# Cross-attention on one core: G x by seven block products, with y's low parts later on GpSimd

## The reference

```python
x_q = jnp.einsum('oc,bcn->bno', w_qk, y)
x_k = jnp.einsum('oc,bcn->bon', w_qk, x)
x_v = jnp.einsum('oc,bcn->bon', w_v, x) + b_v[None, :, None]
energy = jnp.einsum('bnc,bcm->bnm', x_q, x_k)
attention = jax.nn.softmax(energy, axis=-1)
attention = attention / (1e-07 + attention.sum(axis=1, keepdims=True))
x_r = jnp.einsum('bcn,bnm->bcm', x_v, attention)
x_r = jax.nn.relu(jnp.einsum('oc,bcn->bon', w_t, x - x_r) + b_t[None, :, None])
return x + x_r
```

## Time and profile before

| | value |
|---|---|
| median of 3 runs | 1847.62 us (1847.48 to 1848.41) |
| profiled execution, span | 1846.8 us |
| PE busy | 1841.7 us, 100% |
| VectorE (DVE) busy | 1499.5 us, 81% |
| ScalarE (ACT) busy | 1310.9 us, 71% |
| GpSimd (POOL) busy | 788.0 us, 43% |
| bytes moved | 101.92 MB, mean 55 GB/s |

### The profile page before, as it was taken

The page is one execution under the profiler, slowest core; times in us unless marked ns, Lnnn a source line. Parts: engine busy times, 40 slices in busy tenths (PEclk is TensorE's granted clock), DMA queues, the critical chain, the costliest instruction groups (busy, mean ns, idle before and its releaser), DMA issues.

```text
span 1846.8 us, 26440 instructions
## 1 busy us (share of the span) xinstructions
PE 1841.7 (100%) x8901; PEld 1553.5 (84%) x8901; DVE 1499.5 (81%) x2034; ACT 1310.9 (71%) x1799; POOL 788.0 (43%) x422
## 2 busy tenths in 40 slices
PE   9999999999999999999999999999999999999999
PEld 8888888888888888888888888888888888888887
DVE  7878787787887877878878788787787877878777
ACT  7767776677666786667776677766677666776665
POOL 5543344432444424444244452444533444334431
PEclk9999999999999999999999999999999999999999
DMA  3201111011110111101111111111011110111101
GB/s 108 68 25 57 58 68 68 23 68 46 68 68 23 68 46 68 68 33 58 46 68 68 48 43 46 68 68 61 30 48 66 68 68 23 64 50 68 68 1 46
DMA packets 34090, 101.92 MB, mean 55 GB/s; under 512 B 4224, under 2 KB 5248, under 8 KB 34048
## 3 DMA queue, kind: packets, MB, share of 16 engines
q1 hardware_dynamic: 33760, 101.07, 15.8%
q10 hardware_dynamic: 288, 0.39, 0.1%
HBM read 67.90 MB, written 33.55 MB: 55 GB/s over the span
## 4 chain that ended last, share of the span: by engine, by line
PE 98%; DVE 1%; ACT 0%; issue 0%; POOL 0%; DVEq 0%; ACTq 0%; POOLq 0%
PE pv L796 37%; PE row_b L691 19%; PE row_a L691 14%; PE pv L768 9%; PE row_b L754 5%; PE row_a L754 5%; PE row_a L745 5%; PE row_b L745 5%; DVE colsum L536 0%; PE pv L898 0%; PE pv L754 0%; PE pv L931 0%; PE pv L902 0%; ACT p_sb L336 0%; DVE z_lo L503 0%
## 5 line engine op out<-in xcount | busy, mean ns | idle before, releaser
L218 POOL TENSOR_TENSOR y_lo<-y_raw,y_hi 128x896 fp32r<-128x896 f32 (+1 forms) x128 | 277.1, 2190 | 546.7 <-ACT y_hi L297 357.1
L543 DVE SCALAR_TENSOR_TENSOR p_lo<-p_sb,row_inv,p_hi 128x1024 fp32r<-128x1024 f32 x254 | 325.4, 1282 | 96.0 <-ACT p_hi L344 95.9
L327 ACT ACTIVATE ev<-row_b 128x512 f32<-128x512 f32 x384 | 229.5, 598 | 199.7 <-PE row_b L691 199.1
L203 POOL TENSOR_TENSOR x_lo<-x_sb,x_hi 128x1024 fp32r<-128x1024 f32 x63 | 152.2, 2415 | 449.2 <-ACT x_hi L280 449.2
L336 ACT ACTIVATE p_sb<-p_sb,neg_max 128x1024 f32<-128x1024 f32 x256 | 295.1, 1154 | 28.6 <-DVE neg_max L518 24.6
L344 ACT ACTIVATE p_hi<-p_sb,row_inv 128x1024 fp32r<-128x1024 f32 x256 | 292.4, 1143 | 30.7 <-PE pv L796 30.0
L536 DVE SCALAR_TENSOR_TENSOR colsum<-p_sb,row_inv,colsum 128x1024 f32<-128x1024 f32 x224 | 291.7, 1302 | 8.5 <-DVE row_inv L526 0.6
L796 PE MATMUL pv<-p_hi,z_hi 128*128 128x512 f32 x1024 | 273.7, 389 | 0.0
L796 PE MATMUL pv<-p_hi,z_lo 128*128 128x512 f32 x1024 | 273.7, 389 | 0.0
L518 DVE CUSTOM_DVE_ANT_0 p_sb<-row_a,ev 128x1024 f32<-128x1024 f32 x128 | 156.6, 1223 | 143.6 <-PE row_a L691 143.6
L796 PE MATMUL pv<-p_lo,z_hi 128*128 128x512 f32 (+1 forms) x1047 | 271.7, 383 | 0.0
(11 more groups left out here) (157 smaller groups left out, 3585.9 us busy)
## 6 DMA issues: line engine op xcount, KB each, us to landing
x_sb<-x SPq DMA_DIRECT2D x64, 512.0 KB, 4.6
out<-res SPq DMA_DIRECT2D x62, 512.0 KB, 3.4
y_raw<-y SPq DMA_DIRECT2D x64, 256.0 KB, 3.7
y_raw<-y SPq DMA_DIRECT2D x32, 512.0 KB, 3.7
out<-res SPq DMA_DIRECT2D x2, 256.0 KB, 2.1
res<-w_qk SPq DMA_DIRECT2D x1, 256.0 KB, 3.0
res<-w_t_T SPq DMA_DIRECT2D x1, 256.0 KB, 6.7
res<-w_v SPq DMA_DIRECT2D x1, 256.0 KB, 7.8
```

The source lines that it names most:

```text
L218: nc.gpsimd.tensor_tensor(y_lo[:, of:, cols], y_raw[:, 1 + of:8, cols], y_hi[:, of:, cols].bitcast(FP32), ALU.subtract).then_inc(y_lo_done, 1)
L327: nc.scalar.activation(ev[:, to, :], bank_b, ACT.Copy, scale=scale).then_inc(b_copied, 1)
L543: nc.vector.scalar_tensor_tensor(out=p_lo[r][:, :], in0=p_sb[r][:, :], scalar=row_inv[:, j:j + 1], in1=p_hi[r][:, :].bitcast(FP32), op0=AL ...
```

## The change

G x is computed by seven block products of three matmuls each, 21 matmuls of 512 columns where there were 24. For that:

- Once, in batch 0, ScalarE and GpSimd make seven 128 x 128 operands from G and their low parts (`g_operands_high`, `g_operands`). ScalarE's part stands in pair 0 ahead of the first exponentials, and its last instruction waits for all five of GpSimd's sums.
- Four sums of blocks of x are made by DMA: SyncE loads four blocks (`load_xt`) behind the next y, and GpSimd's queue issues three accumulating transfers (`xt_one`, `xt_two`, `xt_four`), each behind a wait for the one before. ScalarE makes their high parts (`xt_high`, in pairs 2 and 3), GpSimd their low parts (`xt_low`, two of 128 x 1024, behind the two `x_low`).
- The seven products stand among the last pair's `pv_pass`. Four PSUM copies on ScalarE (`gx_pass`) carry a partial result from bank to bank, and VectorE adds two (`gx_add`) ahead of `gx_parts`. PE waits for these copies at `gx_p6`, `gx_p3`, `gx_p7` and `gx_p4`. `gx_p5` waits for both `xt_low`.
- GpSimd makes `y_low` of tiles 1 to 3 last in its batch, behind `t_low`, and without the wait for the last `p_low`. `y_sums` of the next batch stands behind `xt_one`, which waits for the four x blocks.
- To make room, `x_sb` is single: x comes once into `x_raw` (over which `x_lo` is written) and again into `x_sb` (`keep_x`, behind the store of the batch before), and `x_bias` moves from pairs 0 and 1 to pairs 1 and 2. `turn` writes over `p_sb[0]` and `colsum`, and stands ahead of the last `p_low`. `scale(b, 1)` stands behind the first `z_low`.

```diff
+            def load_xt(b):
+                for block, kt, cols in ((X_T1, 0, left), (X_T3, 1, right), (X_T2, 1, right), (X_T4, 1, left)):
+                    sp.dma_start(xt_raw[:, block, :], x_dram[b][:, kt, cols]).then_inc(xt_in, DMA)
...
-                        load_x(b + 1, 1 - par, t)
+                        keep_x(b, t)
+                if not last:
+                    if not first:
+                        sp.wait_ge(w_done, KT * b)
+                    for kt in range(KT):
+                        load_x(b + 1, 1 - par, kt)
 
...
+            def xt_one(b):
+                pool.wait_ge(xt_in, 4 * DMA * b)
+                shared = x_dram[b][:, 0, right].rearrange("p (a n) -> p a n", a=1).to_broadcast([P, 2, BANK])
+                pool.dma_start(xt_raw[:, X_T1:X_T3 + 1, :], shared,
+                               accum_op=ALU.add).then_inc(xt1_added, DMA)
...
+            def xt_two(b):
+                pool.wait_ge(xt1_added, DMA * b)
+                pool.dma_start(xt_raw[:, X_T2, :], xt_raw[:, X_T1, :],
+                               accum_op=ALU.add).then_inc(xt2_added, DMA)
...
+            def xt_four(b):
+                pool.wait_ge(xt2_added, DMA * b)
+                pool.dma_start(xt_raw[:, X_T4, :], xt_raw[:, X_T2, :],
+                               accum_op=ALU.add).then_inc(xt4_added, DMA)
...
+            def xt_low(b, h):
+                pool.wait_ge(xt_hi_done, 2 * (b - 1) + h + 1)
+                two = slice(2 * h, 2 * h + 2)
+                nc.gpsimd.tensor_tensor(xt_lo[:, two, :], xt_raw[:, two, :],
+                                        xt_hi[:, two, :].bitcast(FP32), ALU.subtract).then_inc(xt_lo_done, 1)
...
                 if not last:
+                    xt_one(b + 1)
                     y_sums(b + 1)
+                    xt_two(b + 1)
+                    if b == 0:
+                        g_operands()
...
                     y_low(b + 1, 0)
+                    xt_four(b + 1)
                     for kt in range(KT):
                         x_low(b + 1, 1 - par, kt)
-                    pool.wait_ge(p_lo_done, NT * (b + 1))
-                    for t in range(1, NP):
-                        y_low(b + 1, t)
+                    for h in range(2):
+                        xt_low(b + 1, h)
                     t_three(b + 1)
                     t_low(b + 1, 0)
                     t_low(b + 1, 1)
-
-            nc.gpsimd.memset(zeros[:, :], 0.0).then_inc(zeros_made, 1)
+                    for t in range(1, NP):
+                        y_low(b + 1, t)
...
+            def xt_high(b, h):
+                if h == 0:
+                    act.wait_ge(xt1_added, DMA * b)
+                else:
+                    act.wait_ge(xt4_added, DMA * b)
+                two = slice(2 * h, 2 * h + 2)
+                nc.scalar.activation(xt_hi[:, two, :], xt_raw[:, two, :],
+                                     ACT.Copy).then_inc(xt_hi_done, 1)
...
+                act.wait_ge(g_summed, 5)
+                nc.scalar.activation(gs_hi[:, G_S1:G_NS4 + 1, :], g_sums, ACT.Copy).then_inc(gs_hi_done, 1)
...
+            def gx_pass(b, to, of, done, count, scale):
+                act.wait_ge(done, count)
+                nc.scalar.activation(to, of, ACT.Copy, scale=scale).then_inc(gx_passed, 1)
...
                 if t >= 2 and not last:
                     x_high(b + 1, 1 - par, t - 2, early=first)
+                    xt_high(b + 1, t - 2)
...
+                if t == 0 and first:
+                    g_operands_high()
...
-                if t < 2 and not first and (t == 1 or not last):
-                    x_bias(b, par, t)
-                if t == 0 and last:
+                if 0 < t < 3 and not first and (t == 2 or not last):
+                    x_bias(b, t - 1)
+                if t == 1 and last:
...
+                if t == NP - 1 and not last:
+                    gx_pass(b + 1, gx11, gx22, gx22_part, 3 * b + 1, -1.0)
+                    gx_pass(b + 1, ev[:, 3, :], gx12, gx12_part, b + 1, 1.0)
+                    gx_pass(b + 1, ev[:, 2, :], gx22, gx22_part, 3 * b + 2, 1.0)
                 if t == NP - 1:
                     p_high(b, t, 1, first)
...
+                    gx_high_one(b + 1)
+                    gx_pass(b + 1, gx21, gx22, gx22_part, 3 * b + 3, -1.0)
                     y_high(b + 1, 2)
-                    gx_high(b + 1)
+                    y_high(b + 1, 3)
+                    gx_high_two(b + 1)
```

```diff
+            def gx_add(b):
+                dve.wait_ge(gx12_full, b)
+                dve.wait_ge(gx_passed, 4 * b - 1)
+                nc.vector.tensor_tensor(gx12, gx12, ev[:, 2, :], ALU.add).then_inc(gx_added, 1)
+                dve.wait_ge(gx_passed, 4 * b)
+                nc.vector.tensor_tensor(gx22, gx22, ev[:, 3, :], ALU.add).then_inc(gx_added, 1)
...
                 if b < B - 1 or t < NP - 1:
                     p_low(b, t, 0)
+                if b < B - 1 and t == NP - 1:
+                    turn(b)
+                if b < B - 1 or t < NP - 1:
                     p_low(b, t, 1)
...
+                gx_add(b + 1)
                 gx_parts(b + 1)
                 col_inverse(b)
                 scale(b, 0)
+                z_low(b + 1, 0)
                 scale(b, 1)
-                z_low(b + 1, 0)
                 z_low(b + 1, 1)
...
+            def gx_p5(b):
+                pe.wait_ge(xt_lo_done, 2 * b)
+                pe.wait_ge(gs_lo_done, 1)
+                sum_product(gx12, G_S1, X_T1, True).then_inc(gx12_part, 1)
...
+            def gx_p6(b):
+                pe.wait_ge(gx_passed, 4 * b - 3)
+                sum_product(gx22, G_NS2, X_T2, False).then_inc(gx22_part, 1)
...
+            def gx_p4(b):
+                pe.wait_ge(gx_passed, 4 * b)
+                sum_product(gx21, G_22, X_T4, False).then_inc(gx21_full, 1)
...
-                for n in range(3):
-                    pv_pass(b, t - 1, 1, n)
+                if t == NP - 1 and not last:
+                    pv_pass(b, t - 1, 1, 0)
+                    gx_p1(b + 1, 1 - par)
+                    gx_p5(b + 1)
+                    pv_pass(b, t - 1, 1, 1)
+                    gx_p6(b + 1)
+                    gx_p2(1 - par)
+                    pv_pass(b, t - 1, 1, 2)
+                    gx_p3(b + 1, 1 - par)
+                    gx_p7(b + 1)
+                    pv_pass(b, t, 0, 0)
+                    gx_p4(b + 1)
+                else:
+                    for n in range(3):
+                        pv_pass(b, t - 1, 1, n)
...
-                    next_pair(b, t, first)
-                if not last:
-                    pe.wait_ge(x_lo_done, KT * (b + 2))
-                    pe.wait_ge(max_done, NT * (b + 1))
-                    for k in range(4):
-                        g_block(1 - par, k)
```

198 lines of the change are left out of this document (143 added, 55 removed).

## The result

The changed kernel takes **2258.16 us** (median of 4 runs, 2255.38 to 2259.35), the one before 1847.6 beside it: ratio 1.2221, 95% interval 1.2203 to 1.2238. It is 22% slower. I had said 2127, from 1975 to 2230: the direction is right, the time is above the range. The profiled execution spans 2253.6 us.

What follows compares the result with a forecast made beforehand. PE, busy 1841.7 of 1846.8 us, was taken as the bound. A batch: -0.68 + 4.2 + 4.4 + 0.6 = +8.5 us, 255 in 30 batches; batch 0 adds 24: 2126, with 0.8 2127 us; range 1975 to 2230.

Steps and rivals of the forecast that it cites:

- Full price of a wait: On PE, busy 1841.7 of 1846.8 us: every new wait of PE costs its full length.
- B: At gx_p5, PE waits for GpSimd's two xt_low: 3.95 us, 4.4 in steady batches; bounds 2.65 and 4.0.
- A: At the next batch's first y_high, y's sums on GpSimd come 5.7 us late; PE waits 4.2, bounds 1.1 to 4.5.
- C: At gx_p4, PE waits for ScalarE's fourth pass: 0.6 us a batch, bounds 0 and 0.7.
- the start: In batch 0, ScalarE's first exponential stands behind g_operands_high: 20 us longer, bounds 15 and 25.
- a rival, which shared 0.22 with slow transfers: PE falls to 1.2 GHz pace behind wait B, about 3 us a batch: 2220, from 2150 to 2300; chance 0.22 shared.
- Its own sign of being wrong: On PE: the forecast is wrong if matmuls start 0.45 us apart behind the waits.
- Slack at z of 0.2 us: Ahead of z_half, VectorE's adds and parts take 5.0 of 5.2 us; anything later there is late for z.
- The chained transfers: GpSimd's accumulating transfers cost nothing: 5 us and more each to spare, if they take what loads take.
- Lighter waits: GpSimd and VectorE don't obstruct each other, transfers are quick: 4.0 us a batch, 1986, from 1955 to 2060; chance 0.20.
- few waits: One of the waits at gx_p5 and y_high is away: 1850 to 1955 us; chance 0.05.
- faster: GpSimd is in time at gx_p5 and the other waits are covered: -21 us, 1826.5; chance 0.03.

Runs made afterwards that it cites:

- kernels with the guard: Changed kernel, xt_low and y_low moved earlier, GpSimd waiting for the last p_low before y_low: 1967.72 us; G-sums copy also later, 1956.81; fourth pass also earlier, 1951.53.
- the kernel before with a late `x_low`: Kernel before the change, with GpSimd's second x_low of each batch made three times: 1980.02 us; made four times: 2087.47 us.
- y's sums first: Changed kernel with y's four sums ahead of xt_one on GpSimd, nothing else: 2149.79 us, ratio 1.1638.
- the best version: Changed kernel, xt_low and y_low earlier, GpSimd waiting for the last p_low before y_low, G-sums copy later, fourth pass earlier: 1951.53 us, ratio 1.0561.
- both moved, start and pass: Changed kernel, first xt_low and y_low earlier, G-sums copy in pair 2 of batch 0, fourth pass ahead of gx_high_one: 2077.02 us, ratio 1.1237.

## Why the prediction was right in its direction and too low

- **Full price of a wait: right.** Its own table of waits came near, in the places named: B 3.65 us (4.4 taken, bounds 2.65 to 4.0 and 0.4), A 117 us or 3.9 a batch (4.2 taken; 88.0 + 9.3 + 8.0 + what is left of 33.4 without 21.7), C 0.5 (0.6), the start 21.7 (20). With these alone the sum would give 1846.8 - 21.1 + 267.6 = 2093, 33 under the forecast.
- **The step that failed is the pace.** The sum took all 8808 matmuls at 0.227 us, as if every wait cost its length alone; they ran 160.3 us longer. The forecast knew this as a rival, which shared 0.22 with slow transfers, at 3 us a batch and 2220. It is 5.2: 2.0 behind B, 2.1 behind the waits at a pair's first product (A's are most of them), and some 1.1 more at the short waits and the ends of all stretches, where a first matmul takes 0.50 instead of 0.39 and the last one before runs out uncovered. (The kernels with the guard show that last part alone: clock 0.993 to 0.998, PE busy 1863.5 to 1870.9, still 43 to 50 above 1820.6.) Two things were wrong in the rival's size. It counted a stretch behind wait B only, where there are two. And as a chance it was a case beside the others, though its condition, a long wait B in each batch, was the forecast itself: who predicts the waits has to predict the clock. 2126 for the span, 33 off for the shorter waits and 160 for the pace, is the measured 2253.6. Its own sign of being wrong, starts 0.45 us apart behind the waits, came at 0.43. What this sum doesn't say: with the pace restored, the time falls by 53 behind B and by 4 behind A. The waits and the pace add up to the time, but not each of them can be bought back.
- **The Trainium skill** (TensorE: Matmul & The Clock Gate, What's actually happening) has an idle array fall to half clock. The trace agrees: 0.56 granted in 642 to 648, starts 0.43 us apart, behind a wait of 3.6 us, and the same pace behind waits of 2.5 in the kernel before with a late `x_low`. The two kernels whose repeated waits ahead of z are 0.7 and 1.4 us show 0.993 and 0.998 over the run, and 1.00 from 100 to 1950 us.
- **Wait A: right in mechanism, near in size.** ScalarE waited 6.4 us thirty times (5.7, with bounds of 2.6 and 6 that don't follow from their terms: the quickest are 540.6 + 3.7 + 0.33 + 5.2, 2.8 late, the slowest 545.6 + 1.29 + 6.9, 6.7 late). The last issue of x's blocks was at about 601.6 and GpSimd went on at 608.24, 6.6 us later where 4.5 was taken; the stretch 600 to 612 moved 313 and 376 GB/s with DMA shares of 0.95 and 1.02. The issue by GpSimd, which no row showed, is listed at 1.22 and held GpSimd for 0.8 until its next start (1.0 taken). The four sums took 6.5 (6.9 taken). It is y's own late loads and longer sums for one half and the queue behind x's for the other (y's sums first: 6.4 to 3.0). PE met it at VectorE's maximum, not at `p6` of pair 2 as I had it.
- **Wait B: right, the sharing a little less than taken.** 2.65 without the column sums, as the lower bound says, 3.65 with them, 3.95 taken. The 0.4 that A should have added isn't there.
- **"Slack at z of 0.2 us": right, and worth more than a clause.** It didn't decide the changed kernel. It decided every repair of it: 0.7, 3.5 and 1.4 us a batch came up there.
- **The chained transfers: harmless to this kernel, as said, though the first took twice the 5 us and more that it had.** They landed 10.6 us (from x) and 3.3 us (within SBUF) after their issue; GpSimd stood 3.7 us a batch for the first (110.8), which no wait of PE's shows.
- **Lighter waits, few waits, faster:** wrong in their conditions. In steady batches the two engines do hold each other up, and no wait was covered.

## What to carry to other kernels

If a change makes TensorE wait 2.5 us or more once a batch, put the half pace into the sum from the start: here 1.5 to 2.7 us for each such wait as the mean of a run, on top of the wait, and no more behind 5.8 us than behind 2.5. Then ask whether what follows that wait is on the chain that ended last: only there does a faster pace shorten the time (53 us at B, 4 at A). Ask of each instruction that moves on GpSimd not only when its result is due but which of VectorE's instructions with two inputs in SBUF it will lie beside; a wait that keeps them apart was worth 86 us here. And before a matmul is taken out of an engine that is 100% busy at 21 us in all, add up what its replacement needs on the engines at 81%: VectorE's busy time rose from 1499.5 to 1656.3 us in the best version, and the wait that was left there, ahead of z, is for VectorE.

## What the runs showed of the hardware that I had not expected

- A VectorE instruction with two SBUF inputs can be held through several GpSimd instructions in a row, not one: `p_lo` of 1.28 us took 5.62 (608.74), beside sums that began at 609.02, 610.27, 611.51 and 613.34. I had taken it that each waits for one whole instruction of the other. The mean `colsum` of the changed kernel is 2093 ns where it was 1302, the mean `p_lo` 1728 where it was 1282.
- The half pace costs about the same behind a wait of 2.5 us (1.7 a batch) and of 5.8 us (1.8). In the changed kernel it is 2.0 behind B as a mean, but from 0.1 to 3.0 behind waits of nearly one length: one of 3.7 us cost 0.1, others 1.5 to 3.0. With both moved, start and pass, waits of 3.7 cost 2.7 as a mean. What decides it within a run stays open.
- The granted clock fell behind repeated waits of 2.5 us, and not behind repeated waits of 1.4 us (1.00 from 100 us on). Between the two there are only scattered waits.
